# The token list of a mixture-of-experts router: wide comparisons with broadcast operands replaced by narrow ones with a scalar per partition

## The chip, the cores and the metric

The kernel runs on one core of one Trainium2 chip. The metric is the device time of one execution in microseconds; a median of several runs is given. A profiled execution has a time of its own, beside which its trace is read. The engines are TensorE (PE in the profile; its weight loads are PEld), VectorE (DVE), ScalarE (ACT), GpSimd (POOL) and SyncE (SP), which issues most of the DMAs.

## What is computed

Two layers on 4096 tokens of 128 values. Each layer is a layernorm, an attention `s`, a mixture of experts `g`, and `x = x + s * silu(g)`. The mixture of experts of layer 0, cut to what matters here (layer 1 has no capacity and another gelu):

```python
probs = jax.nn.softmax(xf @ Wg, axis=-1)          # 4096 tokens, 8 experts
topv, topi = jax.lax.top_k(probs, 2)
gates = topv / jnp.sum(topv, axis=-1, keepdims=True)
eidx = topi.reshape(-1)
oh = jax.nn.one_hot(eidx, e, dtype=jnp.int32)
pos = jnp.sum(jnp.cumsum(oh, axis=0) * oh, axis=-1) - 1
keep = pos < cap
h = jax.nn.gelu(jnp.einsum('ecd,edh->ech', expert_in, W1) + b1[:, None, :])
y = jnp.einsum('ech,ehd->ecd', h, W2) + b2[:, None, :]
out = (gathered * w).reshape(n, K, d).sum(axis=1)
```

So each token goes to its two best experts, and for each expert the kernel needs the list of its tokens.

## The kernel before

`build` runs, for each layer, `build_layernorm`, `build_router`, `build_experts` and `build_attention`. Each is a block with one program per engine, and a block ends when all its engines are done. The order of the work on an engine is the order in which it is written; waits between engines are semaphores, written out by hand.

Tokens lie as 32 columns (NT) of 128 partitions. In `build_router` DVE finds each token's two best experts, counts, and gives each of the 2 x 4096 choices a slot number (`slotf`, 64 columns). A slot number is split into a place (the low 7 bits, `placei`) and a tile (the rest, `tilei`, under 72), L532 to L534. The list is the inverse of that: for each slot, which token. It is made by matrix products. For each of the 64 columns there is a one-hot matrix of the places, 128 x 128 (`at_place`), and a matrix with two halves of 72 columns (`numbers`): one-hot of the tile times the token's row (its partition, `R.row_of`), and one-hot of the tile times the token's column (`R.tile_of`). PE multiplies the two and sums over the columns in PSUM (L466).

The 64 columns are taken in 8 chunks of 8 (`CHUNK`, `CHUNKS`), through a ring of 4 buffers (`RING`). Per chunk: DVE compares `tile_b`, broadcast along 72, with `R.steps` 0 to 71, broadcast along 8 (`at_tile`, 576 elements a partition, L542), and `place_b` with `R.steps` 0 to 127 (`at_place`, 1024 elements, L544). ACT multiplies `at_tile` by the row (L484), POOL by the column (L440); both wait for `tile_chunks`. PE waits for `place_chunks`, `row_chunks` and `block_chunks`. When a buffer is used again, its writers wait for `used_chunks`, which PE raises.

Behind its loop DVE works on: in layer 0 `totals` and `keep` (L548 to L551), in both layers `R.slot` (L552), `past` and `owner`, the gates, and last `number_t` and `R.ids` (L569, L570), which read PE's sums and first wait for all eight chunks. In `build_experts` POOL then copies four ids (L642) and fetches rows by them; DVE writes each tile's `result` (L758).

ACT also fills the attention's `stack` buffers in this block (`fill_stack`, L426): sixteen copies in layer 0, nine ahead of the exponential of the gates and seven between its chunks, and four in layer 1, ahead of the exponential. `R.steps` and `R.tile_of` are bf16, `R.row_of` is f32, one value a partition.

Other lines that the prediction speaks of: L206 to L212 are small DVE steps of the layernorm on 128 x 8, L351 copies small masks on POOL, L1431 and L1476 are DVE steps of the attention of layer 1 with a scalar per partition (`R.no_outside`, `R.outside`), and L1479 is a copy behind the latter.

Of the kernel before, what the change touches and what calls it, by code (L numbers as in the profile page):

```python
# [6 lines left out]
ALU = mybir.AluOpType  # L7
ACT = mybir.ActivationFunctionType
# [6 lines left out]
P = 128  # L15
BATCH, SEQ, C = 16, 256, 128
NTOK = BATCH * SEQ
NT = NTOK // P
# [3 lines left out]
EXPERTS, HIDDEN, TOPK = 8, 512, 2  # L22
# [9 lines left out]
TILES = NTOK * TOPK // P + EXPERTS  # L32
# [342 lines left out]
def build_router(nc, R, D, layer):  # L375
# [5 lines left out]
    with ExitStack() as ctx:  # L381
        sem = lambda name: ctx.enter_context(nc.semaphore(f"rt{layer}_{name}"))
        sb = lambda name, shape: ctx.enter_context(nc.sbuf_tensor(f"rt{layer}_{name}", shape, F32))
# [6 lines left out]
        gap = sb("gap", [P, NT])  # L390
# [13 lines left out]
        slotf = sb("slotf", [P, TOPK, NT])  # L404
        sloti, placei, tilei = (ctx.enter_context(nc.sbuf_tensor(f"rt{layer}_{name}", [P, TOPK * NT], I32)) for name in ("sloti", "placei", "tilei"))
        bf = lambda name, shape: ctx.enter_context(nc.sbuf_tensor(f"rt{layer}_{name}", shape, BF16))
        place_b = bf("place_b", [P, TOPK * NT])
        tile_b = bf("tile_b", [P, TOPK * NT])
        CHUNK = 8
        CHUNKS = TOPK * NT // CHUNK  # L410
        RING = 4
        at_place = [bf(f"at_place{q}", [P, CHUNK, P]) for q in range(RING)]
        at_tile = [bf(f"at_tile{q}", [P, CHUNK, TILES]) for q in range(RING)]
        numbers = [bf(f"numbers{q}", [P, CHUNK, 2, TILES]) for q in range(RING)]
        past = sb("past", [1, TILES, E])
        owner = sb("owner", [1, TILES])
        number_t = sb("number_t", [P, TILES])
        chain, gap_ready, gap_exp, chosen_ready, counted, places_ready, place_chunks, tile_chunks, row_chunks, block_chunks, used_chunks = (
            sem(n) for n in ("chain", "gap_ready", "gap_exp", "chosen_ready", "counted", "places_ready", "place_chunks", "tile_chunks", "row_chunks", "block_chunks", "used_chunks"))

        block = ctx.enter_context(nc.Block())
        def fill_stack(copy, i):

            buffer, t = R.stack[i // 4], i % 4
            rows = R.fixed[:, 2 * layer + t % 2, :].unsqueeze(1).broadcast_to([P, SLOTS, SEQ])
            copy(buffer[:, :, t, :], rows)  # L426

        @block.gpsimd
        def _(pool):
            if layer == 0:  # L430
                pool.wait_ge(R.wqk_in, 16 * 6)
                for t in range(6):
                    dst = R.wqk[t // 4][:, t % 4, :].rearrange("p (h g j) -> p h g j", h=2, j=2)
                    nc.gpsimd.tensor_copy(dst, R.wqk_raw[:, t, :].rearrange("p (g h j) -> p h g j", h=2, j=2))
            for c in range(CHUNKS):
                pool.wait_ge(tile_chunks, c + 1)
                if c >= RING:
                    pool.wait_ge(used_chunks, c - RING + 1)
                js = slice(c * CHUNK % NT, c * CHUNK % NT + CHUNK)
                nc.gpsimd.tensor_tensor(numbers[c % RING][:, :, 1, :], at_tile[c % RING][:], R.tile_of[:, js].unsqueeze(2).broadcast_to([P, CHUNK, TILES]),  # L440
                                        ALU.mult).then_inc(block_chunks, 1)

        @block.sync
        def _(sp):
# [11 lines left out]
        @block.tensor  # L456
        def _(pe):
            pe.wait_ge(chosen_ready, 1)
            nc.tensor.matmul(R.ps[:, 1, 0:NT * E], R.before[:], flat(chosen[:]), start=True, stop=True)
            nc.tensor.matmul(R.ps[:, 2, 0:NT * E], R.ones[:], flat(chosen[:]), start=True, stop=True).then_inc(counted, 1)  # L460
            for c in range(CHUNKS):
                pe.wait_ge(place_chunks, c + 1)
                pe.wait_ge(row_chunks, c + 1)
                pe.wait_ge(block_chunks, c + 1)
                for i in range(CHUNK):
                    last = nc.tensor.matmul(R.ps[:, 3, 0:2 * TILES], at_place[c % RING][:, i, :], numbers[c % RING][:, i, :, :].rearrange("p k t -> p (k t)"),  # L466
                                            start=(c == 0 and i == 0), stop=(c == CHUNKS - 1 and i == CHUNK - 1))
                last.then_inc(used_chunks, 1)

        @block.scalar  # L470
        def _(act):
            if layer == 0:
                for i in range(9):
                    fill_stack(nc.scalar.copy, i)
            else:
                for i in range(0, 16, 4):
                    fill_stack(nc.scalar.copy, i)
            act.wait_ge(gap_ready, 1)
            nc.scalar.activation(gap[:], gap[:], ACT.Exp).then_inc(gap_exp, 1)
            for c in range(CHUNKS):  # L480
                act.wait_ge(tile_chunks, c + 1)
                if c >= RING:
                    act.wait_ge(used_chunks, c - RING + 1)
                nc.scalar.activation(numbers[c % RING][:, :, 0, :], at_tile[c % RING][:], ACT.Copy, scale=R.row_of[:, 0:1]).then_inc(row_chunks, 1)  # L484
                if layer == 0 and c < 7:
                    fill_stack(nc.scalar.copy, 9 + c)

        @block.vector
        def _(dve):
            n = [0]  # L490

            def link(ins):
                n[0] += 1
                ins.then_inc(chain, 1)
                dve.wait_ge(chain, n[0])
# [20 lines left out]
            for e in range(E):  # L516
                last = nc.vector.tensor_tensor_scan(upto[:, :, e], ones[:], totals[:, :, e], 0.0, ALU.mult, ALU.add)
# [14 lines left out]
            link(nc.vector.tensor_copy(sloti[:], slotf[:].rearrange("p k t -> p (k t)")))  # L532
            nc.vector.tensor_scalar(placei[:], sloti[:], P - 1, None, ALU.bitwise_and)
            link(nc.vector.tensor_scalar(tilei[:], sloti[:], 7, None, ALU.logical_shift_right))  # L534
            nc.vector.tensor_copy(place_b[:], placei[:])
            nc.vector.tensor_copy(tile_b[:], tilei[:]).then_inc(places_ready, 1)
            dve.wait_ge(places_ready, 1)
            for c in range(CHUNKS):
                if c >= RING:
                    dve.wait_ge(used_chunks, c - RING + 1)  # L540
                js = slice(c * CHUNK, (c + 1) * CHUNK)
                nc.vector.tensor_tensor(at_tile[c % RING][:], tile_b[:, js].unsqueeze(2).broadcast_to([P, CHUNK, TILES]),  # L542
                                        R.steps[:, 0:TILES].unsqueeze(1).broadcast_to([P, CHUNK, TILES]), ALU.is_equal).then_inc(tile_chunks, 1)
                nc.vector.tensor_tensor(at_place[c % RING][:], place_b[:, js].unsqueeze(2).broadcast_to([P, CHUNK, P]),  # L544
                                        R.steps[:].unsqueeze(1).broadcast_to([P, CHUNK, P]), ALU.is_equal).then_inc(place_chunks, 1)
            if layer == 0:

                link(nc.vector.tensor_scalar(totals[:], place[:], float(CAP), None, ALU.is_lt))  # L548
# [960 lines left out]
def build(nc, D):  # L1509
    D["xn_rows"] = nc.dram_tensor("xn_rows", (NTOK, C), F32).ap()  # L1510
    D["list_out"] = nc.dram_tensor("list_out", (LISTED * P, C), F32).ap()
    with ExitStack() as ctx:
# [44 lines left out]
        for layer in range(2):  # L1557
            with ExitStack() as until_experts:
                R.weights = until_experts.enter_context(nc.sbuf_tensor(f"weights{layer}", [P, EXPERTS, WIDTH], F32))
                if layer == 0:  # L1560
                    R.wqk_raw = until_experts.enter_context(nc.sbuf_tensor("wqk_raw", [P, 6, C], F32))
                build_layernorm(nc, R, D, layer)
                build_router(nc, R, D, layer)
                build_experts(nc, R, D, layer)
            build_attention(nc, R, D, layer)
# [37 lines left out]
```

## Time and profile before

| | us |
|---|---|
| median of 3 runs | 1352.54 (1351.52 to 1356.94) |
| span of the profiled execution | 1353.5 |
| PE busy in it | 1071.2 |
| DVE busy | 809.8 |
| ACT busy | 799.8 |
| POOL busy | 615.5 |
| PE's matmuls of the token list (L466, 128 of them) | 17.9 |
| DVE's `at_tile` (L542, 16) | 25.3 |
| DVE's `at_place` (L544, 16) | 19.4 |
| POOL's products (L440, 16) | 33.0 |
| ACT's products (L484, 16) | 12.4 |

A busy time is the time in which an engine had an instruction under way. Instructions of one engine can overlap a little: the time from one start to the next (here called the pitch) is shorter than the duration where nothing is waited for. A share of the span says little where the stages follow one another; a stage is read from the timeline, by what each engine waited for there.

### The profile page before, as it was taken

The page shows a single profiled execution, that of the slowest core. Times are in us where ns is not written, and L with a number is a line of the kernel's source. Part 1 is how long each engine was busy: PE and PEld are TensorE (multiplying, and loading weights), DVE is VectorE, ACT ScalarE, POOL GpSimd, SP SyncE. Part 2 cuts the span into 40 slices and gives each one's busy share as a digit, 9 for nine tenths or more (in the row PEclk, how much of TensorE's full clock was granted, in tenths as well). Part 3 has the DMA queues.
Part 4 walks back from the last instruction along what each step waited for, and adds up shares of the span by engine and source line. Part 5 has one row for each costly group of instructions (what it writes and reads, how often), then busy time and mean ns, then how long its engine had stood idle before and what let it go on. Part 6 is the DMA issues. An engine that isn't in the chain of part 4 may idle for free. (4 is left out here: it accounts for less than half of the span.)

```text
span 1353.5 us, 38128 instructions
## 1 busy us (share of the span) xinstructions
PE 1071.2 (79%) x12376; PEld 808.5 (60%) x12376; DVE 809.8 (60%) x1668; ACT 799.8 (59%) x1892; POOL 615.5 (45%) x918
## 2 busy tenths in 40 slices
PE   4359998588999798899987344999857888978885
PEld 3349998355565455556554244999824655655553
DVE  4676664568777577777751357666436664755641
ACT  4845555057777677777776342655514665656663
POOL 6256553023455456555665416655303242444443
PEclk9999999579999899999998555999958898989997
DMA  6402222322332222232200340222212122222210
GB/s 181 113 24 69 70 69 47 93 56 58 85 77 58 58 57 65 67 85 68 57 20 9 94 109 16 71 69 68 55 47 63 44 64 66 55 62 64 52 48 20
DMA packets 144615, 86.43 MB, mean 64 GB/s; under 512 B 16547, under 2 KB 138037, under 8 KB 144469
## 3 DMA queue, kind: packets, MB, share of 16 engines
q1 hardware_dynamic: 135828, 66.72, 18.9%
q0 software_dynamic: 8640, 17.71, 5.6%
q8 instruction: 98, 1.61, 0.5%
q14 instruction: 49, 0.39, 0.1%
HBM read 30.06 MB, written 15.60 MB: 34 GB/s over the span
## 5 line engine op out<-in xcount | busy, mean ns | idle before, releaser
L1424 DVE TENSOR_REDUCE at_maxima<-ps 128x2 f32<-128x512 f32 (+1 forms) x576 | 371.7, 683 | 226.3 <-PE ps L1117 223.9
L1313 ACT ACTIVATE at_probs<-ps 128x512 f32<-128x512 f32 x576 | 320.8, 598 | 108.8 <-PE ps L1117 104.2
L1116 PE MATMUL ps<-tables 64*128 64x256 bf16 (+1 forms) x2304 | 229.6, 260 | 128.9 <-DMA stack<-at_pieces 62.3
L1117 PE MATMUL ps<-stack 62*128 62x256 bf16 (+3 forms) x3072 | 265.6, 255 | 2.4 <-issue 2.4
L717 ACT ACTIVATE ex_hid<-ps,ex_w 128x128 f32<-128x128 f32 x568 | 162.0, 368 | 120.3 <-PE ps L690 111.2
L1116 PEld LDWEIGHTS ps<-tables 64*128 64x128 bf16 x2304 | 91.7, 96 | 229.7 <-issue 193.9
L646 POOL DMA_INDIRECT ex_rows<-xn_rows,ex_ids_now x142 | 143.7, 1012 | 110.4 <-PE ps L681 68.7
L1117 PEld LDWEIGHTS ps<-stack 62*128 62x128 bf16 (+1 forms) x3072 | 167.1, 99 | 13.7 <-issue 2.6
L750 DVE COPY ex_w<-weights 128x1156 f32 x142 | 109.3, 769 | 103.8 <-issue 102.8
L1005 POOL DMA_INDIRECT at_chosen_y<-list_out,at_slot x128 | 130.1, 1017 | 55.3 <-issue 29.0
L690 PE MATMUL ps<-ex_rowsT,ex_w 128*128 128x128 f32 x1136 | 154.8, 281 | 0.0
L701 PE MATMUL ps<-ex_w,ex_hid 128*128 128x128 f32 x1136 | 150.6, 276 | 1.1 <-DVE ex_result L758 1.1
L690 PEld LDWEIGHTS ps<-ex_rowsT,ex_w 128*128 128x128 f32 x1136 | 141.3, 196 | 1.2 <-issue 0.2
L701 PEld LDWEIGHTS ps<-ex_w,ex_hid 128*128 128x128 f32 x1136 | 138.7, 193 | 1.4 <-issue 1.4
L1207 PE MATMUL ps<-at_probs,at_v 128*32 128x256 f32 x1536 | 131.4, 416 | 3.3 <-ACT at_probs L1313 3.3
L1026 POOL TENSOR_TENSOR at_s_rows<-at_s_rows,at_silu 128x256 f32<-128x256 f32 x32 | 23.2, 726 | 183.3 <-ACT at_s_rows L1365 183.3
L950 POOL COPY at_xb<-xnT 128x256 f32<-128x256 f32 (+1 forms) x32 | 15.9, 498 | 155.4 <-PE ps L1108 97.8
L1210 PE MATMUL ps<-at_probs,at_v 128*32 128x128 f32 x1536 | 81.7, 286 | 0.0
L1210 PEld LDWEIGHTS ps<-at_probs,at_v 128*32 128x32 f32 x1536 | 52.7, 117 | 38.3 <-issue 8.8
L1098 PE MATMUL ps<-xnT,wqk 128*128 128x256 f32 (+1 forms) x192 | 63.6, 449 | 9.6 <-POOL at_v L1034 9.3
L1318 ACT COPY at_weighed_t<-ps 128x512 f32<-128x512 f32 x96 | 56.7, 591 | 14.7 <-PE ps L1210 12.2
L1218 PE MATMUL ps<-ident,at_weighed_t 128*128 128x128 f32 x384 | 63.7, 291 | 0.1
(188 smaller groups left out, 1504.2 us busy)
## 6 DMA issues: line engine op xcount, KB each, us to landing
stack<-at_pieces SPq DMA_DIRECT2D x192, 128.0 KB, 2.7
stack<-at_pieces SPq DMA_DIRECT2D x192, 64.0 KB
list_out<-ex_result SPq DMA_DIRECT2D x142, 64.0 KB, 1.5
weights<-in_L_w SPq DMA_DIRECT2D x4, 1024.0 KB, 5.6
weights<-in_L_w SPq DMA_DIRECT2D x16, 256.0 KB, 6.6
xn_rows<-xn SPq DMA_DIRECT2D x8, 512.0 KB, 3.3
ex_rows<-xn_rows,ex_ids_now POOLq DMA_INDIRECT x142, 2.6
x<-in_L_attn_x SPq DMA_DIRECT2D x4, 512.0 KB, 6.1
```

The lines of the kernel that those rows point to most:

```text
L646: nc.gpsimd.indirect_dma_start(rows[q][:], None, D["xn_rows"], bass.IndirectOffsetOnAxis(ids[:, q:q + 1], 0)).then_inc(loaded[q], 16)
L690: last = nc.tensor.matmul(hid_ps[q % 2][:, hb * P:(hb + 1) * P], w[q][:, W1 + hb * P:W1 + (hb + 1) * P], rowsT[q % 2][:], start=True, stop ...
L701: last = nc.tensor.matmul(out_ps[q % 2][:, 0:C], hid[q % 2][:, hb, :], w[q][:, W2 + hb * C:W2 + (hb + 1) * C], start=(hb == 0), stop=(hb = ...
L717: last = nc.scalar.activation(hid[q % 2][:, hb, :], hid_ps[q % 2][:, hb * P:(hb + 1) * P], gelu, bias=w[q][:, B1 + hb:B1 + hb + 1])
L750: nc.vector.tensor_copy(w[q][:], weights[:, bass.ds(e, 1), :].rearrange("p o w -> p (o w)"))
L1005: nc.gpsimd.indirect_dma_start(chosen_y[t][k][:], None, D["list_out"], bass.IndirectOffsetOnAxis(slot[:, i:i + 1], 0)).then_inc(gathered, 16)
L1116: return nc.tensor.matmul(fine(bank, j), R.eye[tile, j, :], mask[tile], start=(j == 0), stop=True, skip_group_check=(j > 0))
L1117: return nc.tensor.matmul(bank[:, j - 2, :], left(j - 2)[tile], right(j - 2)[tile], start=False, stop=True, skip_group_check=True)
L1207: nc.tensor.matmul(strip, v[p][:, 0, h, :], pr[:, part, at:at + SEQ], start=True, stop=False)
L1210: last = nc.tensor.matmul(strip[:, P:SEQ], v[p][:, 1, h, :], pr[:, 2, at:at + P], start=False, stop=True)
L1313: nc.scalar.activation(probs[:, (n // 3) % 2, n % 3, i * 512:(i + 1) * 512], t_bank[i], ACT.Exp, scale=SCALE).then_inc(t_free, 1)
L1424: nc.vector.tensor_reduce(by_half[:, h0:h0 + heads, a], s_bank[i].rearrange("p (m k) -> p m k", k=P * (late + 1)), AX.X, ALU.max).then_inc ...
```

## The change

The two wide DVE comparisons of a chunk, ACT's product and POOL's product go. In their place there is, for each of the 8 columns of a chunk, one `tensor_scalar` per matrix: it compares `R.steps` with the column's place or tile, which is now a scalar per partition from `place_f` or `tile_f` (f32), and for `numbers` it multiplies in the same operation: by the row (a second scalar per partition), or by the column number (a constant). POOL makes the column halves of the first 4 columns (`BY_POOL`) of each chunk, DVE all the rest. POOL waits for `places_ready` once and for the ring; it no longer waits for DVE in each chunk. In ACT's program the exponential comes ahead of the four fills of layer 1, and the last seven fills of layer 0 come behind it in one run.

```diff
-        place_b = bf("place_b", [P, TOPK * NT])
-        tile_b = bf("tile_b", [P, TOPK * NT])
+        place_f = sb("place_f", [P, TOPK * NT])
+        tile_f = sb("tile_f", [P, TOPK * NT])
...
+        BY_POOL = 4
+
+        def number_blocks(eng, c, i):
+
+            j = c * CHUNK + i
+            return eng.tensor_scalar(numbers[c % RING][:, i, 1, :], R.steps[:, 0:TILES], tile_f[:, j:j + 1], float(j % NT), ALU.is_equal, ALU.mult)
...
+            pool.wait_ge(places_ready, 1)
             for c in range(CHUNKS):
-                pool.wait_ge(tile_chunks, c + 1)
                 if c >= RING:
                     pool.wait_ge(used_chunks, c - RING + 1)
-                js = slice(c * CHUNK % NT, c * CHUNK % NT + CHUNK)
-                nc.gpsimd.tensor_tensor(numbers[c % RING][:, :, 1, :], at_tile[c % RING][:], R.tile_of[:, js].unsqueeze(2).broadcast_to([P, CHUNK, TILES]),
-                                        ALU.mult).then_inc(block_chunks, 1)
+                for i in range(BY_POOL):
+                    last = number_blocks(nc.gpsimd, c, i)
+                last.then_inc(block_chunks, 1)
...
                 pe.wait_ge(place_chunks, c + 1)
-                pe.wait_ge(row_chunks, c + 1)
                 pe.wait_ge(block_chunks, c + 1)
...
-            else:
+            act.wait_ge(gap_ready, 1)
+            nc.scalar.activation(gap[:], gap[:], ACT.Exp).then_inc(gap_exp, 1)
+            if layer:
                 for i in range(0, 16, 4):
                     fill_stack(nc.scalar.copy, i)
-            act.wait_ge(gap_ready, 1)
-            nc.scalar.activation(gap[:], gap[:], ACT.Exp).then_inc(gap_exp, 1)
-            for c in range(CHUNKS):
-                act.wait_ge(tile_chunks, c + 1)
-                if c >= RING:
-                    act.wait_ge(used_chunks, c - RING + 1)
-                nc.scalar.activation(numbers[c % RING][:, :, 0, :], at_tile[c % RING][:], ACT.Copy, scale=R.row_of[:, 0:1]).then_inc(row_chunks, 1)
-                if layer == 0 and c < 7:
-                    fill_stack(nc.scalar.copy, 9 + c)
+            if layer == 0:
+                for i in range(9, 16):
+                    fill_stack(nc.scalar.copy, i)
...
-            nc.vector.tensor_copy(place_b[:], placei[:])
-            nc.vector.tensor_copy(tile_b[:], tilei[:]).then_inc(places_ready, 1)
+            link(nc.vector.tensor_copy(place_f[:], placei[:]))
+            nc.vector.tensor_copy(tile_f[:], tilei[:]).then_inc(places_ready, 1)
             dve.wait_ge(places_ready, 1)
...
-                js = slice(c * CHUNK, (c + 1) * CHUNK)
-                nc.vector.tensor_tensor(at_tile[c % RING][:], tile_b[:, js].unsqueeze(2).broadcast_to([P, CHUNK, TILES]),
-                                        R.steps[:, 0:TILES].unsqueeze(1).broadcast_to([P, CHUNK, TILES]), ALU.is_equal).then_inc(tile_chunks, 1)
-                nc.vector.tensor_tensor(at_place[c % RING][:], place_b[:, js].unsqueeze(2).broadcast_to([P, CHUNK, P]),
-                                        R.steps[:].unsqueeze(1).broadcast_to([P, CHUNK, P]), ALU.is_equal).then_inc(place_chunks, 1)
+                for i in range(BY_POOL, CHUNK):
+                    number_blocks(nc.vector, c, i)
+                for i in range(CHUNK):
+                    j = c * CHUNK + i
+                    nc.vector.tensor_scalar(numbers[c % RING][:, i, 0, :], R.steps[:, 0:TILES], tile_f[:, j:j + 1], R.row_of[:, 0:1], ALU.is_equal, ALU.mult)
+                    last = nc.vector.tensor_scalar(at_place[c % RING][:, i, :], R.steps[:], place_f[:, j:j + 1], None, ALU.is_equal)
+                last.then_inc(place_chunks, 1)
```

## Rows read from the trace of the kernel before

**Rows 1.** Timeline, loop's start: start us, us, engine, line, operation, out<-in, count [idle before<-releaser].
```profile
56.66 0.76 DVE L542 TENSOR_TENSOR rt_at_tile<-rt_tile_b,steps 128x576 bf16<-128x576 bf16 x1
57.33 1.22 DVE L544 TENSOR_TENSOR rt_at_place<-rt_place_b,steps 128x1024 bf16<-128x1024 bf16 x1
57.50 2.06 POOL L440 TENSOR_TENSOR rt_numbers<-rt_at_tile,tile_of 128x576 bf16<-128x576 bf16 x1 [8.68 <-DVE rt_at_tile L542]
...
58.47 1.70 DVE L542 TENSOR_TENSOR rt_at_tile<-rt_tile_b,steps 128x576 bf16<-128x576 bf16 x1
...
60.09 1.21 DVE L544 TENSOR_TENSOR rt_at_place<-rt_place_b,steps 128x1024 bf16<-128x1024 bf16 x1
...
60.25 2.06 POOL L440 TENSOR_TENSOR rt_numbers<-rt_at_tile,tile_of 128x576 bf16<-128x576 bf16 x1 [0.69 <-DVE rt_at_tile L542]
```

**Rows 2.** Timeline, loop's end in layer 0; then L552's durations, min/median/max in ns.
```profile
77.76 1.23 DVE L548 TENSOR_SCALAR rt_totals<-rt_place 128x256 f32<-128x256 f32 x1
...
78.98 1.12 PE L466 MATMUL ps<-rt_numbers,rt_at_place 128*128 128x144 bf16 x8 [1.63 <-POOL rt_numbers L440]
...
83.86 0.23 DVE L569 TENSOR_SCALAR rt_number_t<-ps 128x72 f32<-128x72 f32 x1
...
L552 DVE CAST slot<-rt_slotf x2: 199/666/1132, 80.8 to 828.2; 128x64 uint32<-128x64 f32 x2
```

**Rows 3.** Timeline, small DVE steps of the layernorm of layer 0, POOL idle.
```profile
14.94 0.17 DVE L206 TENSOR_TENSOR ln_within<-ln_stats 128x8 f32<-128x8 f32 x1
15.03 0.16 DVE L207 TENSOR_TENSOR ln_spread<-ln_stats 128x8 f32<-128x8 f32 x1
...
15.66 0.17 DVE L212 SCALAR_TENSOR_TENSOR ln_var<-ln_spread,ln_within 128x8 f32<-128x8 f32 x1
15.75 1.63 DVE L202 BATCH_NORM_STATS2 ln_stats<-x 128x6 f32<-128x128 f32 x8
```

**Rows 4.** Timeline around L1476; then durations of L1431 and L523, min/median/max in ns.
```profile
1055.71 0.24 DVE L1476 SCALAR_TENSOR_TENSOR at_rsum<-at_zero_exp,outside,at_weighed_q 128x16 f32<-128x16 f32 x1
1055.86 0.17 DVE L1479 COPY at_rsum<-at_weighed_q 128x16 f32<-128x16 f32 x1
...
L1431 DVE TENSOR_SCALAR at_maxima<-at_maxima,no_outside x16: 233/272/445, 1008.8 to 1309.0; 128x16 f32<-128x16 f32 x16
...
L523 DVE TENSOR_SCALAR rt_tiles<-rt_tiles x2: 171/172/172, 51.9 to 802.4; 128x8 f32<-128x8 f32 x2
```

**Rows 5.** Timeline, the two integer operations that split the slot numbers, layer 0.
```profile
55.99 0.20 DVE L533 TENSOR_SCALAR rt_placei<-rt_sloti 128x64 int32<-128x64 int32 x1
56.10 0.19 DVE L534 TENSOR_SCALAR rt_tilei<-rt_sloti 128x64 int32<-128x64 int32 x1
```

**Rows 6.** One line's instructions, L351, from 17.4 to 18.6 us; then DVE's timeline there.
```profile
L351 POOL COPY tables<-const_fine x6: 226/226/227, 17.6 to 18.4; 64x64 bf16<-64x64 bf16 x6
...
17.42 0.17 DVE L206 TENSOR_TENSOR ln_within<-ln_stats 128x8 f32<-128x8 f32 x1
...
18.38 0.17 DVE L212 SCALAR_TENSOR_TENSOR ln_var<-ln_spread,ln_within 128x8 f32<-128x8 f32 x1
```

**Rows 7.** Timeline, ACT's first nine fills of layer 0.
```profile
41.26 16.30 ACT L426 COPY stack<-tables 128x2048 bf16<-128x2048 bf16 x9 [2.89 <-PEq L172]
```

**Rows 8.** Timeline, first ids in each layer; then L758's instructions, first and last start.
```profile
84.62 0.19 POOL L642 COPY ex_ids_now<-ids 128x4 uint32<-128x4 uint32 x1 [5.79 <-POOLq L381]
...
832.93 0.18 POOL L642 COPY ex_ids_now<-ids 128x4 uint32<-128x4 uint32 x1 [3.61 <-POOLq L381]
...
L758 DVE TENSOR_TENSOR ex_result<-ps,ex_w x71: 270/283/292, 95.5 to 228.6; 128x128 f32<-128x128 f32 x71
L758 DVE TENSOR_TENSOR ex_result<-ps,ex_w x71: 271/284/293, 843.3 to 976.7; 128x128 f32<-128x128 f32 x71
```

**Rows 9.** Windows: stretch, length, busy us (instructions) of each engine, PEclk, DMA share, GB/s.
```profile
57.00:80.00 23.00, 8.85 (x64) 6.83 (x64) 22.90 (x20) 19.29 (x17) 16.49 (x8) 1.00 0.19 38
...
837.00:841.00 4.00, 3.15 (x14) 2.91 (x15) 2.26 (x5) 0.46 (x2) 2.81 (x4) 0.50 0.19 53
```

More of the change, by code:

```diff
@@ L412, in build_router @@
         at_place = [bf(f"at_place{q}", [P, CHUNK, P]) for q in range(RING)]
-        at_tile = [bf(f"at_tile{q}", [P, CHUNK, TILES]) for q in range(RING)]
         numbers = [bf(f"numbers{q}", [P, CHUNK, 2, TILES]) for q in range(RING)]
@@ L417, in build_router @@
         number_t = sb("number_t", [P, TILES])
-        chain, gap_ready, gap_exp, chosen_ready, counted, places_ready, place_chunks, tile_chunks, row_chunks, block_chunks, used_chunks = (
-            sem(n) for n in ("chain", "gap_ready", "gap_exp", "chosen_ready", "counted", "places_ready", "place_chunks", "tile_chunks", "row_chunks", "block_chunks", "used_chunks"))
+        chain, gap_ready, gap_exp, chosen_ready, counted, places_ready, place_chunks, block_chunks, used_chunks = (
+            sem(n) for n in ("chain", "gap_ready", "gap_exp", "chosen_ready", "counted", "places_ready", "place_chunks", "block_chunks", "used_chunks"))
         block = ctx.enter_context(nc.Block())
```

## The prediction

> **What bounds the kernel now.** I first read the page's busy shares and its 40 slices: no engine is busy all the time, and the kernel runs as stages that follow one another (layernorm, router, experts, attention, twice). So the change is worth what it makes of its own stage, the router's token list, provided that the next stage waits for it. The timeline of that stage is the view that decides.
>
> In the loop over eight chunks the starts of one wide comparison `at_place` and the next are 57.33 and 60.09, a period of 2.76 us [rows 1]. Within it three operations stand in a row and never overlap. `at_place` takes 1.21. POOL's product is recorded for 2.06, but it starts 0.17 into `at_place` and ends at 59.56, which is 1.0 after `at_place` ended. The next `at_tile` starts at 58.47 and ends at 60.17, 0.6 after POOL's end; the first one, which had no POOL work beside it, took 0.76 instead of 1.70. So a POOL operation and a DVE operation with two tensors in SBUF wait for each other as wholes, and the period is 1.14 of `at_place`, 1.0 of POOL and 0.6 of `at_tile`. ACT and PE are not in it: PE's eight matmuls take 1.12 and wait for POOL [rows 2].
>
> The loop costs DVE 77.76 - 56.66 = 21.1 us a layer [rows 1, 2]. The first DVE step behind it is blocked by POOL's last product as well: `totals` takes 1.23 in layer 0, and the cast of `slot` takes 1.13 in layer 1 against 0.20 where it is free [rows 2]. After that DVE goes on without a wait to the ids, while PE finished at 80.1, 3.8 us ahead of the step that reads its sums [rows 2]. The experts begin right behind the ids. Every microsecond of the DVE loop is therefore on the path, in both layers, and PE has cover.
>
> **The change part by part.** Removed are 2 wide DVE operations, 1 wide POOL operation and 1 ACT operation per chunk. Added per chunk are 20 narrow DVE operations (12 of 72 elements, 8 of 128) and 4 POOL operations of 72.
>
> *The price of a wide element.* The two wide forms have pitches of 0.67 (576 elements) and 1.14 (1024) where POOL is out of the way [rows 1]. The difference gives 1.05 ns an element, and 0.065 us remains per operation.
>
> *The price of a narrow operation.* Operations of 8 elements with constants start every 0.09 us [rows 3], so 0.065 is confirmed. But each new operation takes a scalar per partition from SBUF, and there is one row for that: the `scalar_tensor_tensor` of L1476, 16 elements, is followed by the next operation 0.15 after its start, and its duration is 0.24 against 0.17 for the same operation with a constant [rows 3, 4]. The `tensor_scalar` of L1431 says the same: at least 233 ns with such a scalar, 172 for one with a constant [rows 4]. Such a scalar costs 0.06 to 0.07 us of the engine's time. This is the choice that decides the sign. Without its 16 elements the operation costs 0.133.
>
> *The rate of its data.* No row shows a dense 2-byte `tensor_scalar`. The nearest is the integer `tensor_scalar` of 64 elements, pitch 0.11, 0.02 to 0.03 more than 8 elements cost: some 0.5 ns an element [rows 5]. Ends: no cost beyond the 16-element row gives 20 x 0.15 = 3.0 us a chunk; 0.5 ns gives 12 x 0.169 + 8 x 0.197 = 3.6; the wide operations' 1.05 ns gives 12 x 0.209 + 8 x 0.267 = 4.65. I take 3.3, halfway between the first two, since the new data are 2-byte and contiguous, half the bytes of the row. Eight chunks: 26.4 us.
>
> On this the Trainium skill ("VectorE: DVE Perf Modes", "Mode 4×_2P") says that a one-source operation on contiguous 16-bit data in SBUF runs four elements a cycle; an estimate from its 0.96 GHz is 0.26 ns an element, and the sum would be 3.15 a chunk. No row here shows that rate.
>
> *POOL beside it.* 32 POOL operations a layer. Six small copies in a row on POOL start every 0.16 us. While they ran, the chain of small DVE steps from `within` to `var` took 18.38 - 17.42 = 0.96, against 15.66 - 14.94 = 0.72 with POOL idle: 0.24 for five copies, 0.05 each [rows 3, 6]. 32 x 0.05 = 1.6 us. Bounds are nothing and a whole POOL operation each time, 32 x 0.226 = 7.2. I take 1.6, since the row has the same size of operations on both engines. POOL is not the pace: four operations at 0.2 to 0.4 are under 3.3, and it may run three chunks ahead.
>
> *The link between the two casts.* The second cast now waits for the first: a full 0.20 instead of a pitch of 0.11 [rows 5], +0.1.
>
> *Behind the loop.* POOL is finished long before DVE, so `totals` and `slot` are no longer blocked: 1.13 - 0.20, -0.9 a layer [rows 2].
>
> *ACT.* Its scaled copy goes, and seven of the sixteen stack fills of layer 0 now stand in one run behind the exponential. Nine took 16.30 from 41.26 [rows 7]; seven more at 1.81 end near 70.4, while the experts start at 84.62 [rows 8], so 14 us cover it. In layer 1 the fills wait for the exponential's input, some 6 us later than now, and end 25 us before ACT is next wanted. Nothing for either. If the cover were gone, each would cost what sticks out.
>
> *PE.* Each chunk keeps its eight matmuls, and one wait falls away. The last ones end some 1.3 us after DVE's last comparison; DVE reads the sums 3 us or more after it. Nothing.
>
> **The sum.** Per layer 26.4 + 1.6 - 21.1 + 0.1 - 0.9 = +6.1; twice, +12.2. The profiled execution spans 1353.5, which would become 1365.7; the median of the runs shown is 1.0 lower, so I forecast 1364.7.
>
> **The rivals.**
>
> *The scalar is free (faster).* The engine could fetch the next operation's scalar while the present one streams, in a run where every operation has one. The only pitch I have is followed by a copy that has none. For it: nothing in a row forbids it. Against it: the duration itself is longer, and in two kinds of operation. It decides at a scalar price of about 0.03 us, half of the row's. Then 20 x 0.068 = 1.36 a chunk goes: 1.94 x 8 = 15.5, and 15.5 + 1.6 - 21.1 - 0.8 = -4.8 a layer: 1343 (1348 with 0.5 ns an element).
>
> The Trainium skill ("Vector Engine (DVE) Microarchitecture Reference", "Measured stream behaviour on trn2") gives about 75 ns per instruction plus the stream and no extra for a scalar; an estimate by it and by four elements a cycle is 2.0 us a chunk, which is this rival. Rows 4 speak against it.
>
> *Half hidden.* Scalars partly overlapped, or free with more blocking by POOL: a chunk of about 2.5 to 2.8, 1348 to 1358, no change.
>
> *The second scalar costs too.* The eight row-number operations take two of them, and no row has two. At 0.068 more each: 0.54 a chunk, 4.4 a layer, 1373.
>
> *POOL blocks as a whole.* As in the present loop, each POOL operation could hold DVE for its 0.226: 7.2 instead of 1.6, +5.6 a layer, 1376. For it: rows 1. Against: rows 6, at the new sizes.
>
> The Trainium skill ("SBUF — State Buffer", "Who interferes with whom") states that an operation in a 2-port mode and a GpSimd operation exclude each other for the whole instruction. Rows 1 agree with exclusion, for operations of two inputs; by it this rival would hold in full.
>
> *The data run at the wide rate.* 4.65 a chunk: 1386.
>
> *The clock.* PE's matmuls get sparser, and the granted clock, 1.00 through 57 to 80 us, that is 2.4 GHz [rows 9], could fall in layer 0 before the experts. Layer 1's experts started at 0.50, 1.2 GHz, still so at 837 to 841 [rows 9], and took from their first ids to their last result 976.7 - 832.9 = 143.8 us against 228.6 - 84.6 = 144.0 in layer 0 [rows 8]. A fall costs nothing there.
>
> **How the numbers follow.** 0.42 for the forecast; 0.25 for the three dearer cases together (second scalar 0.12, POOL 0.10, wide rate 0.03); 0.20 for the free scalar; 0.13 for half hidden. A measurement of this kernel tells 0.5% from no change, 1345.8 to 1359.3. Faster takes two thirds of the free scalar, 0.14. No change takes the rest of it, the half hidden case and a small part of the forecast's lower bound, 0.22. Slower is 0.64. The forecast's own range, from 3.0 to 3.6 a chunk, is 1360 to 1370. The full range reaches to the free scalar and to POOL's whole blocking, 1344 to 1377; with the upper bound of both dear cases left out, some 0.2 stays outside.
>
> **What would show it.** The narrow operations' pitch on DVE: 0.16 to 0.17 means the forecast, 0.09 to 0.11 the free scalar, and a longer one only at the row numbers the second scalar. Durations: about 0.23 to 0.25 each. The loop from the first narrow operation to `totals`: 28 us instead of 21.1. `totals` at 0.3 and `slot` at 0.20. POOL's 32 operations far ahead of DVE's. The experts' and attention's stages should keep their lengths. I am wrong if the loop is under 22 us, or if a later stage moves by more than 2 us.

## The result

The changed kernel takes 1371.6 us, median of 4 runs (1368.71 to 1374.1), beside 1353.94 for the kernel before in the same comparison. The ratio is 1.0124 (95% interval 1.0099 to 1.0149): slower by 16.8 us, within 13.4 to 20.2. The forecast was 1364.7, +12.2, with a full range of 1344 to 1377. The sign was right and the size somewhat short: the forecast's own range, 1360 to 1370, was missed by 1.6.

The profiled execution spans 1369.3 us, 15.8 more than before. The timeline shows where they are. Columns as in rows 1; these are the loop's first column pairs of layer 0, a chunk from which POOL has gone (layer 1), and the loop's end in layer 0.

```profile
56.80 0.69 DVE L432 TENSOR_SCALAR rt_numbers<-steps,rt_tile_f 128x72 bf16<-128x72 bf16 x4
56.87 13.16 POOL L432 TENSOR_SCALAR rt_numbers<-steps,rt_tile_f 128x72 bf16<-128x72 bf16 x22 [8.21 <-DVE rt_tile_f L537]
57.40 0.30 DVE L546 TENSOR_SCALAR rt_numbers<-steps,rt_tile_f,row_of 128x72 bf16<-128x72 bf16 x1
...
57.60 0.25 DVE L547 TENSOR_SCALAR rt_at_place<-steps,rt_place_f 128x128 bf16<-128x128 bf16 x1
57.62 12.68 ACT L425 COPY stack<-tables 128x2048 bf16<-128x2048 bf16 x7
57.77 0.30 DVE L546 TENSOR_SCALAR rt_numbers<-steps,rt_tile_f,row_of 128x72 bf16<-128x72 bf16 x1
...
839.42 0.68 DVE L432 TENSOR_SCALAR rt_numbers<-steps,rt_tile_f 128x72 bf16<-128x72 bf16 x4
840.01 0.29 DVE L546 TENSOR_SCALAR rt_numbers<-steps,rt_tile_f,row_of 128x72 bf16<-128x72 bf16 x1
840.22 0.24 DVE L547 TENSOR_SCALAR rt_at_place<-steps,rt_place_f 128x128 bf16<-128x128 bf16 x1
840.38 0.29 DVE L546 TENSOR_SCALAR rt_numbers<-steps,rt_tile_f,row_of 128x72 bf16<-128x72 bf16 x1
...
842.98 0.68 DVE L432 TENSOR_SCALAR rt_numbers<-steps,rt_tile_f 128x72 bf16<-128x72 bf16 x4
...
86.54 0.28 DVE L551 TENSOR_SCALAR rt_totals<-rt_place 128x256 f32<-128x256 f32 x1
86.68 1.14 PE L471 MATMUL ps<-rt_numbers,rt_at_place 128*128 128x144 bf16 x8 [2.42 <-DVE rt_at_place L547]
...
92.46 0.19 POOL L645 COPY ex_ids_now<-ids 128x4 uint32<-128x4 uint32 x1 [16.35 <-POOLq L381]
```

Read the pitches first. In the chunk without POOL the four block operations take 840.01 - 839.42 = 0.59, 0.147 each. Then come eight pairs of 0.37: 0.21 for the row operation, which has two scalars per partition, and 0.16 for the place. A chunk is 842.98 - 839.42 = 3.56 us. With POOL beside it the loop of layer 0 takes 86.54 - 56.80 = 29.7 us, against 21.1 before [rows 1, 2]. `totals` now takes 0.28 instead of 1.23 [rows 2]. The first ids copy is at 92.46 instead of 84.62 [rows 8]: +7.8 us. ACT's seven fills end at 70.3, and PE waits for DVE.

The next rows are one line's instructions (durations in ns, min/median/max, first and last start), and then windows with columns as in rows 9.

```profile
L432 POOL TENSOR_SCALAR rt_numbers<-steps,rt_tile_f x64: 522/529/716, 56.9 to 835.2; 128x72 bf16<-128x72 bf16 x64
L761 DVE TENSOR_TENSOR ex_result<-ps,ex_w x71: 270/283/292, 103.9 to 236.9; 128x128 f32<-128x128 f32 x71
L761 DVE TENSOR_TENSOR ex_result<-ps,ex_w x71: 270/283/291, 861.6 to 994.7; 128x128 f32<-128x128 f32 x71
...
57.00:86.00 29.00, 8.00 (x56) 5.97 (x56) 29.00 (x157) 13.30 (x9) 17.15 (x32) 1.00 0.15 30
```

A POOL operation takes 0.53 us, and the last starts 11 us ahead of the loop's end in layer 1 (835.2; the loop ends at 846.5). The granted clock stays at 1.00 (2.4 GHz) through layer 0's loop, though PE is busier before [rows 9]. From the first ids copy to the last result the experts of layer 0 take 236.9 - 92.5 = 144.4 us, 144.0 before [rows 8]. Over both layers the router's stage, from its first DVE step to the first ids copy, is 7.8 and 8.0 us longer, which is the whole of the 15.8. That the two agree to a tenth is in part luck: the stretch from layer 0's first ids to layer 1's router is 1.5 us longer than before, and the one behind layer 1's first ids 1.5 shorter.

### The profile page after: what moved, and what is told of

The parts are those of the page before. It is cut to its first block and busy times, and to the rows that moved or that the text cites. A ratio compares the mean times of both kernels' runs of the same rounds, so it can differ in the third digit from the quotient of the medians.

```text
span 1369.3 us, 38432 instructions
## 1 busy us (share of the span) xinstructions
PE 1075.0 (79%) x12376; PEld 810.8 (59%) x12376; DVE 825.6 (60%) x1956; ACT 788.1 (58%) x1876; POOL 614.9 (45%) x966
## 5 line engine op out<-in xcount | busy, mean ns | idle before, releaser
L471 PE MATMUL ps<-rt_numbers,rt_at_place 128*128 128x144 bf16 x128 | 18.3, 324 | 58.9 <-DVE rt_at_place L547 58.9
```

## The experiments

Each kernel was measured beside the kernel before, and has a name by which the text calls it. Besides its ratio I give the change of the stage: from DVE's first router step to the first ids copy, both layers added, in the profiled execution. It is the sharper number. Two profiled executions can differ by several us elsewhere: from the first ids copy of layer 0 to the start of layer 1's router the kernels below took 704 to 710 us, in no order that goes with their edits.

### The changed kernel without the second scalar (`one_scalar`)

```diff
-tensor_scalar(numbers[c % RING][:, i, 0, :], R.steps[:, 0:TILES], tile_f[:, j:j + 1], R.row_of[:, 0:1], ALU.is_equal, ALU.mult)
+tensor_scalar(numbers[c % RING][:, i, 0, :], R.steps[:, 0:TILES], tile_f[:, j:j + 1], 1.0, ALU.is_equal, ALU.mult)
```

> The changed kernel, with the constant 1.0 in place of the row number as second scalar per partition in the 64 row-number operations of each layer (the row numbers of the list are therefore not computed; all else is). Theory (each scalar per partition costs DVE 0.06 us, the second as much as the first): the pitch of these operations falls from 0.205 to 0.147 us, DVE's loop from 29.8 to about 26.1 us a layer, the whole by some 7.5 us, to about 1364. Rival (they are dear because they alternate with the 128-element ones, or because POOL blocks them): pitch and loop stay, about 1371.

Measured: 1362.7 us, ratio 1.0061 (1.0037 to 1.0084). Stage +6.5 us instead of +15.8. The row operation, start to start with the place operation behind it, is 0.15 us:

```profile
60.76 0.29 DVE L546 TENSOR_SCALAR rt_numbers<-steps,rt_tile_f 128x72 bf16<-128x72 bf16 x1
60.91 0.24 DVE L547 TENSOR_SCALAR rt_at_place<-steps,rt_place_f 128x128 bf16<-128x128 bf16 x1
61.07 0.23 DVE L546 TENSOR_SCALAR rt_numbers<-steps,rt_tile_f 128x72 bf16<-128x72 bf16 x1
61.22 0.25 DVE L547 TENSOR_SCALAR rt_at_place<-steps,rt_place_f 128x128 bf16<-128x128 bf16 x1
```

So the second scalar costs as much as the first, though it is the same value in every operation while the first changes, and alternation has no part in it. The loop of layer 0 fell from 29.7 to 25.2 us, 0.7 more than 64 scalars explain. That rest is POOL's share: chunks without POOL take 3.08 here, so POOL costs DVE 25.2 - 8 x 3.08 = 0.6 us instead of 1.3, 0.02 for each of its operations. Why it is less here the runs don't show.

### All on DVE, with the scalars and without any (`no_pool`, `no_pool_no_scalar`)

```diff
-        BY_POOL = 4
+        BY_POOL = 0
```

with POOL's loop and PE's wait for it left out. The second kernel also has -1.0 for `tile_f[:, j:j + 1]` and `place_f[:, j:j + 1]`, and 1.0 for the row; it makes no list.

> The changed kernel, with POOL's four operations of each chunk on DVE as well, so that POOL does nothing in the loop. Theory (POOL costs DVE only 0.04 us per POOL operation, 1.3 us a layer): DVE gains 32 operations of 0.147, loses 1.3, so the loop grows from 29.8 to 33.1 us a layer and the whole to about 1378. Rival (POOL and DVE exclude each other as in the kernel before, so POOL's operations cost DVE most of their own time): loop at most 30 us, 1371 or less.

> As no_pool, and every scalar per partition is replaced by the constant -1.0, so that no comparison is true: the same 24 operations a chunk with the same shapes and types, and no list (every slot gets token 0). Theory (the scalar is what makes them dear): pitches of about 0.085 us (72 elements) and 0.10 (128), loop 17.3 us a layer instead of 33.1, whole about 1344 to 1346, faster than the kernel before. Rival (a small operation costs its 0.14 whatever its scalar is, or its data run at 1 ns an element): loop over 26 us, 1364 or more.

Measured: 1373.1 us, ratio 1.0148 (1.0116 to 1.018), stage +22.6 (the 1378 expected was 5 too high, while the loop, 33.4 instead of 33.1, was as expected); and 1344.7 us, ratio 0.9928 (0.9906 to 0.9951), stage -8.4. The three kinds of operation, one line's instructions each, first with the scalars, then without (L432 is the block, L538 the row, L539 the place):

```profile
L432 DVE TENSOR_SCALAR rt_numbers<-steps,rt_tile_f x128: 223/236/250, 57.0 to 845.9; 128x72 bf16<-128x72 bf16 x128
L538 DVE TENSOR_SCALAR rt_numbers<-steps,rt_tile_f,row_of x128: 283/297/307, 58.2 to 848.6; 128x72 bf16<-128x72 bf16 x128
L539 DVE TENSOR_SCALAR rt_at_place<-steps,rt_place_f x128: 234/249/259, 58.4 to 848.8; 128x128 bf16<-128x128 bf16 x128
```

```profile
L432 DVE TENSOR_SCALAR rt_numbers<-steps x128: 169/178/189, 56.7 to 821.6; 128x72 bf16<-128x72 bf16 x128
L538 DVE TENSOR_SCALAR rt_numbers<-steps x128: 168/179/191, 57.4 to 823.0; 128x72 bf16<-128x72 bf16 x128
L539 DVE TENSOR_SCALAR rt_at_place<-steps x128: 179/192/201, 57.5 to 823.1; 128x128 bf16<-128x128 bf16 x128
```

One scalar adds 58 and 57 ns to the median, two add 118. Without them the pitches, in the timeline of the second kernel, are:

```profile
60.09 0.18 DVE L539 TENSOR_SCALAR rt_at_place<-steps 128x128 bf16<-128x128 bf16 x1
60.19 0.17 DVE L538 TENSOR_SCALAR rt_numbers<-steps 128x72 bf16<-128x72 bf16 x1
60.27 0.18 DVE L539 TENSOR_SCALAR rt_at_place<-steps 128x128 bf16<-128x128 bf16 x1
```

The means over layer 0 are 0.102 for 128 elements and 0.087 for 72, or 0.26 ns an element and 0.07 besides. From the cast of the tiles to the step behind the loop the two kernels take 33.4 and 18.0 us. The difference, 15.5 us, divided by 8 chunks of 32 scalars, is 0.060 us a scalar. This settles the sign: the same narrow operations with constants make the kernel faster by 10 us. This kernel compares with -1.0 and so finds nothing equal; `one_scalar`, whose comparisons still come true, gives the same price for a scalar. Its experts, which fetch token 0 for every slot, take 144.9 and 145.5 us, hardly more than before. `no_pool` also prices POOL: 33.4 less 32 operations of 0.148 is 28.7, and the changed kernel, with these on POOL, takes 30.0 over the same stretch. Its 32 operations cost DVE 1.3 us, 0.04 each.

### Only one half of the change (`numbers_narrow`, `place_narrow`)

In the first kernel the numbers are narrow and the places wide (its edit against the changed kernel follows); in the second the places are narrow and the rest is as before.

```diff
-    last = nc.vector.tensor_scalar(at_place[c % RING][:, i, :], R.steps[:], place_f[:, j:j + 1], None, ALU.is_equal)
+    nc.vector.tensor_tensor(at_place[c % RING][:], place_b[:, js].unsqueeze(2).broadcast_to([P, CHUNK, P]),
+                            R.steps[:].unsqueeze(1).broadcast_to([P, CHUNK, P]), ALU.is_equal).then_inc(place_chunks, 1)
```

> The changed kernel, with the places compared by one wide operation a chunk as before (1024 elements, 1.14 us) in place of eight narrow ones. Theory (eight narrow ones cost 8 x 0.163 = 1.30): a chunk of 3.4 us, loop about 28.5, whole about 1369, so nearly all of the loss is in the numbers matrix. Rival (the wide operation has two inputs in SBUF and waits for whole POOL operations of 0.53 us, up to one a chunk): loop 29.8 to 32, no gain against the changed kernel.

> The kernel before, with only the places compared by eight narrow operations a chunk; tiles, ACT's and POOL's products as before. Theory: 8 x 0.163 = 1.30 in place of 1.14 and POOL's 1.0 still excludes DVE: chunk 2.9 us against 2.76, loop about 22.5, +2 to +3 us in all. Rival (narrow operations hold the shared port only in part, so that POOL's product runs in their gaps): chunk 2.0 to 2.4, loop 16 to 19, faster than before by 5 to 10 us.

Measured: 1365.6 us, ratio 1.0096 (1.0063 to 1.0129), stage +12.3; and 1358.2 us, ratio 1.0024 (1.0006 to 1.0042), stage +2.9. So the numbers carry four fifths of the loss. In the first kernel a wide comparison of two inputs stands beside POOL's short operations (one line's instructions each, durations in ns):

```profile
L432 POOL TENSOR_SCALAR rt_numbers<-steps,rt_tile_f x64: 517/550/1819, 56.9 to 837.9; 128x72 bf16<-128x72 bf16 x64
L548 DVE TENSOR_TENSOR rt_at_place<-rt_place_b,steps x16: 1206/1210/1216, 59.1 to 839.1; 128x1024 bf16<-128x1024 bf16 x16
```

The wide comparison is never longer than its free 1.21, so it doesn't wait for POOL, and the rival is out (the loop of layer 0 takes 28.0 us); it is POOL that waits, with about one operation a chunk of 1.5 us or more instead of 0.55. The second kernel shows the opposite (its timeline, a chunk of layer 0, then one line's instructions):

```profile
60.35 2.35 DVE L546 TENSOR_SCALAR rt_at_place<-steps,rt_place_f 128x128 bf16<-128x128 bf16 x8
...
60.51 1.16 POOL L440 TENSOR_TENSOR rt_numbers<-rt_at_tile,tile_of 128x576 bf16<-128x576 bf16 x1 [1.77 <-DVE rt_at_tile L542]
...
62.62 0.75 DVE L542 TENSOR_TENSOR rt_at_tile<-rt_tile_b,steps 128x576 bf16<-128x576 bf16 x1
...
L546 DVE TENSOR_SCALAR rt_at_place<-steps,rt_place_f x128: 239/243/1214, 57.4 to 831.3; 128x128 bf16<-128x128 bf16 x128
```

Eight places alone would take some 1.4; they take 2.35, longer by about POOL's 1.0, and the longest single place operation takes 1.214 instead of 0.243. The chunk, 2.94 us, is as expected. POOL's product now ends inside the places and is 1.16 long instead of 2.06 [rows 1]: 0.9 of the old duration was waiting for `at_place`. So this POOL operation, of 1.0 us and two inputs, does stop the run of narrow ones for its whole time, while the operations of 0.53 us and one input cost 0.04 each. Whether the length or the second input makes the difference the runs don't separate.

### POOL's product on DVE, wide, and ACT's order (`act_order`, `wide_no_pool`, `wide_no_pool_fills`)

The first kernel moves only ACT's fills and exponential; the second also makes POOL's product on DVE.

```diff
+                dve.wait_ge(tile_chunks, c + 1)
+                nc.vector.tensor_tensor(numbers[c % RING][:, :, 1, :], at_tile[c % RING][:], R.tile_of[:, cols].unsqueeze(2).broadcast_to([P, CHUNK, TILES]),
+                                        ALU.mult).then_inc(block_chunks, 1)
```

> The kernel before, with only ACT's order changed: the exponential ahead of layer 1's fills, and layer 0's last seven fills behind the eight chunks instead of between them. Theory (ACT has cover): no difference, 1352 to 1356. Rival (the fills or the exponential were or become a bound): more than 3 us either way.

> The kernel before with the ACT order of act_order and POOL's product as a third wide operation on DVE (576 elements, two inputs). Theory (DVE and POOL excluded each other, so POOL's 1.0 us a chunk was DVE's time anyway): chunk 1.14 + 0.67 + 0.67 = 2.48 instead of 2.76, loop 19.5, and totals and slot are not blocked: -2.5 us a layer, about 1349. Rival (the long at_tile of 1.70 had another cause than POOL): chunk about 3.4, about +9 us.

Measured: 1358.4 us, ratio 1.0026 (1.0004 to 1.0047), stage +5.7; and 1357.0 us, ratio 1.0014 (0.9994 to 1.0034), stage +1.5. The chunk of the second kernel is 2.48 us, and `at_tile` is 0.75 long where it was 1.70 [rows 1]:

```profile
61.76 0.75 DVE L536 TENSOR_TENSOR rt_at_tile<-rt_tile_b,steps 128x576 bf16<-128x576 bf16 x1
...
62.43 1.22 DVE L538 TENSOR_TENSOR rt_at_place<-rt_place_b,steps 128x1024 bf16<-128x1024 bf16 x1
...
63.57 0.75 DVE L542 TENSOR_TENSOR rt_numbers<-rt_at_tile,tile_of 128x576 bf16<-128x576 bf16 x1
64.23 0.76 DVE L536 TENSOR_TENSOR rt_at_tile<-rt_tile_b,steps 128x576 bf16<-128x576 bf16 x1
```

So the exclusion is real and moving the work off POOL saves what the sum says, 2.3 us a layer to the ids. But the whole did not get faster, and for both kernels the time that I expected was wrong. The end of layer 0's router in `act_order` shows why:

```profile
77.64 12.68 ACT L426 COPY stack<-tables 128x2048 bf16<-128x2048 bf16 x7
90.58 1.28 ACT L718 ACT_TABLE_LOAD   x1 [0.26 <-PEq L381]
90.59 0.19 POOL L643 COPY ex_ids_now<-ids 128x4 uint32<-128x4 uint32 x1 [11.52 <-POOLq L381]
```

The seven fills stand behind the last of ACT's products, which wait for DVE, and end at 90.3. The block ends with its last engine, and the first ids copy comes at 90.59, 6 us late, though DVE had written the ids by 84.58 (its last step starts at 84.35 and takes 0.23). In the change itself the same order is free only because ACT has no products left to wait for. A third kernel does four fills between the first four products and three behind the last.

> As wide_no_pool, but of layer 0's last seven fills of ACT four stand behind the first four chunks' products and three behind the last, in place of all seven behind the last. Theory (the 4.5 us won in wide_no_pool were given back since seven fills of 1.81 us behind the last product ran 6 us past the ids, and the block ends with its last engine): the first ids copy at about 82.5 us instead of 88.5, whole 4 to 6 us below wide_no_pool, 1350 beside 1354 of the kernel before. Rival (the loss lies in the attention or is chance): no difference to wide_no_pool.

Measured: 1351.9 us, ratio 0.9982 (0.9964 to 1.0). The first ids copy is at 82.57, and the stage -4.4 us instead of +1.5, so the rival is out; the two ratios, 0.9982 and 1.0014, agree with that, though their intervals just overlap.

### The columns innermost (`columns_inner`, `columns_inner_fills`, `places_inner`)

The wide comparisons read one operand with a repeated innermost element. Here the order of the dimensions is turned, so that in every operand eight different values lie side by side.

```diff
-        at_place = [bf(f"at_place{q}", [P, CHUNK, P]) for q in range(RING)]
+        at_place = [bf(f"at_place{q}", [P, P, CHUNK]) for q in range(RING)]
...
-    tensor_tensor(at_place[c % RING][:], place_b[:, js].unsqueeze(2).broadcast_to([P, CHUNK, P]), R.steps[:].unsqueeze(1).broadcast_to([P, CHUNK, P]), ALU.is_equal)
+    tensor_tensor(at_place[c % RING][:], place_b[:, js].unsqueeze(1).broadcast_to([P, P, CHUNK]), steps_wide[:], ALU.is_equal)
```

`at_tile` and `numbers` likewise.

> As wide_no_pool, with the eight columns of a chunk as the innermost dimension of all wide tensors, so that every operand is contiguous in runs of eight 2-byte elements and only the outer dimension is broadcast; a table of 128 x 8 steps is made by POOL at the block's start; PE reads its operands with a stride of 16 bytes. Theory (the wide operations ran at 1.05 ns an element because of the broadcast innermost dimension): 0.5 ns an element, chunk 0.60 + 0.37 + 0.37 = 1.34 us, DVE's loop about 11 us a layer and the whole about 1332, if PE's strided reads don't become the pace (8 matmuls took 1.12). Rival (the rate of two-input operations is 1.05 whatever the layout): as wide_no_pool, about 1349. Second rival (strided weight loads and moving reads are slow): PE's chunk over 2 us and PE ends last.

> columns_inner with the same order of fills. Theory: ACT ends near 76 us and the ids at 75.7, so that the first ids copy comes at about 76.5 instead of 81.2; whole about 1341 to 1342. Rival: as columns_inner, 1346.

> columns_inner_fills with the numbers matrix in its old layout (each column's 144 values contiguous), written from the at_tile of the new layout by a strided read; only at_place and at_tile keep the columns innermost. Theory (PE's chunk of 2.13 us comes from its moving operand's stride, not from the weights'): PE back to 1.12 us a chunk, DVE's third operation back to 0.67, chunk 1.64, DVE is the pace again; ids at about 75.5 in layer 0 and 2.5 us earlier in layer 1, whole about 1339. Rival (the strided weights slow PE): PE's chunk over 1.5 us, no gain. Second rival (a strided read costs DVE and ACT more than 1.05 ns an element): chunk over 2.2, slower than columns_inner_fills.

Measured: 1346.7 us, ratio 0.9939 (0.9919 to 0.996); 1342.8 us, ratio 0.9919 (0.9895 to 0.9943); 1345.6 us, ratio 0.9944 (0.9922 to 0.9966). Their stages are -9.9, -13.5 and -9.9 us. Three lines of the first kernel, then two of the third (durations in ns; L462 is PE's product, L544 `at_place` and L548 the block product there):

```profile
60.70 0.46 DVE L540 TENSOR_TENSOR rt_at_tile<-rt_tile_b,rt_steps_wide 128x576 bf16<-128x576 bf16 x1
61.06 0.69 DVE L542 TENSOR_TENSOR rt_at_place<-rt_place_b,rt_steps_wide 128x1024 bf16<-128x1024 bf16 x1
...
L462 PE MATMUL ps<-rt_numbers,rt_at_place x128: 430/442/448, 58.4 to 820.1; 128*128 128x144 bf16 x128
```

```profile
61.24 0.69 DVE L544 TENSOR_TENSOR rt_at_place<-rt_place_b,rt_steps_wide 128x1024 bf16<-128x1024 bf16 x1
61.84 1.23 DVE L548 TENSOR_TENSOR rt_numbers<-rt_at_tile,tile_of 128x576 bf16<-128x576 bf16 x1
```

The wide comparison of 1024 elements has a duration of 0.69 us instead of 1.21, that of 576 takes 0.46 instead of 0.76: 0.5 ns an element. DVE's chunk is 1.34 us, as expected, until it has to wait for a free buffer. But PE's matmul is 442 ns long instead of 324, a chunk of eight takes it 2.1 us instead of 1.12, and PE ends last: DVE starts on the ids at 75.67, after a wait for PE, and not at some 73. The second rival came true, and 1346.7 stands beside the 1332 expected. With the better order of the fills the ids copy follows at 77.7 instead of 81.2, but not at 76.5: a fill between two of ACT's products holds up PE, which waits for them, and the ids themselves come 1.5 us later, at 77.17. In the third kernel PE is back at 325 ns a matmul, so it was the moving operand's stride and not the weights'; but the strided read makes DVE's block product 1.2 us long instead of 0.75, and ACT's 1.3 instead of 0.77, which gives the gain back. ACT, with products of 1.3 us and fills of 1.9, then ends last in layer 0: the ids copy waits until 80.53, though the ids are written by 79.04. The second kernel is the fastest here, by 11 us below the kernel before (interval 8 to 14) and 28 below the changed one.

## Why the prediction was right, point by point

**The bound.** Right. The stage is on the path whole: its +15.8 us are the span's +15.8. What each kernel above did to the stage it did to the whole, within the interval; for the first five it is +6.5 and +8.3, +22.6 and +20.0, -8.4 and -9.7, +12.3 and +13.0, +2.9 and +3.2 (stage in the profile; ratio times 1353), and the other six agree as well. The reading of the old loop as three operations that exclude each other was confirmed by `wide_no_pool`.

**The scalar per partition.** Right, and it decided the sign. Its price from two rows of another stage [rows 4] was 0.06 to 0.07 us; 0.060 was measured. The free scalar is refuted: it would need pitches of 0.09 to 0.10, which only the kernel without scalars has.

**The second scalar.** Here is the term that was mis-sized. I left it out of the forecast and gave it as a rival, with 4.4 us a layer; it costs 0.0604 x 64 = 3.9, and 4.5 with what POOL gave back. The rival itself, at 1373, is the nearest of all cases to 1371.6. Nothing in the trace excluded it. The likelier reading of "each scalar costs 0.06" was that two cost 0.12, and I should have forecast that.

**The chunk.** 3.3 forecast, 3.56 measured. Without the second scalar, 3.56 - 8 x 0.06 = 3.08, so the rest was 0.22 too high. Some 0.15 of that is the data: 3.3 left 0.34 ns for each of the 1888 elements, and they ran at 0.26, while the nearest row [rows 5] gave 0.5. The remainder is the fixed part, 0.13 with one scalar instead of 0.133. The estimate from the Trainium skill ("VectorE: DVE Perf Modes", "Mode 4×_2P"), 0.26, agrees with the measured rate. This error and the missing second scalar have opposite signs, and it is luck that they partly cancelled. The prediction also says that rows 3 confirm 0.065 for the part of an operation that is paid at any length; 0.09 less eight elements is 0.08 there, and the kernel without scalars gives 0.07.

**POOL.** 1.6 us a layer forecast from five small copies [rows 6], 1.3 measured. Its operations are 0.53 us long, more than the 0.2 to 0.4 that I gave them; they still fit, 19 us in 30. Whole blocking, 32 x 0.53 = 17 us, is refuted for them, and with it the rule of the Trainium skill ("SBUF — State Buffer", "Who interferes with whom") in the form in which the prediction uses it, exclusion for the whole of each POOL operation. The rule agrees with the one long operation of `place_narrow`, with the loop before and with the POOL operations that wait for a wide comparison in `numbers_narrow`. Why 32 short ones of 0.53 us cost only 0.04 each, the runs don't show.

**The rest.** `totals` and `slot` unblocked: 0.95 and 0.93 a layer, forecast 0.9. The link of the casts: 0.13, forecast 0.1. ACT: fills end at 70.3, forecast 70.4, and nothing sticks out; `act_order` shows what it costs where it does, 6 us. PE, clock and experts: no change, as forecast. A slip in the rivals: for "half hidden", 2.5 to 2.8 a chunk give 1352 to 1357 by the prediction's own sum, not 1348 to 1358.

**The sum.** Forecast +6.1 a layer, measured +7.8 and +8.0. The missing 1.8: +3.9 for the second scalar, -1.8 for the rest of the chunk (8 x 0.22), -0.3 for POOL.

## What to carry to other kernels

Price a small DVE operation by its pitch and by what it reads besides its tensors: here 0.07 us fixed, 0.06 more for each scalar per partition, and only then 0.26 ns an element. At 72 to 128 elements the part that doesn't depend on their number is four fifths or more, so a fast data rate wins little, and splitting a wide comparison of 1024 elements into eight with a scalar each loses (8 x 0.163 = 1.30 us against 1.14); turning the layout so that the wide operation itself gets faster won 11 us, until PE's reads paid for it. And look for what a moved instruction waits for, not only how long it is: the same seven fills were free where nothing stood ahead of them and cost 6 us behind a wait.

## What the runs showed of the hardware that I had not expected

Two scalars per partition of one DVE operation are paid one after the other: 57 to 58 ns for the first and 60 for the second. In the trace they lengthen the pitch by as much as the duration.

Within a run of eight, matmuls of 144 moving columns whose elements lie 16 bytes apart start every 262 ns (`columns_inner`) instead of every 120 (`before`, and `places_inner`, where only the weights are strided). It is the same in layer 0, at a granted clock of 1.00 (2.4 GHz), and in layer 1, at 0.50 (1.2 GHz). A stride of 16 bytes in the weights costs next to nothing: in `places_inner` the weight loads are 165 ns long instead of 147, and a run of eight takes 1.15 us instead of 1.12. DVE and ACT pay for the same stride when they read it: 1.18 and 1.35 us (medians) for 576 elements instead of 0.75 and 0.77, some 0.7 and 1.0 ns more an element.

POOL's work and DVE's can wait for each other in either direction. Beside POOL's product of 1.0 us a narrow DVE operation takes up to 1.214 us instead of 0.243; beside DVE's wide comparison of 1.21 us a POOL operation takes up to 1.8 instead of 0.55; and beside runs of narrow DVE operations POOL's short ones cost DVE 0.04 us each.
